# Two attention tails and the cross attention between them, written as one block

## The reference, cut to what matters

```python
def _mha(x, y, ..., causal):
    xn = _ln(x, lnx_g, lnx_b)
    yn = _ln(y, lny_g, lny_b)
    q, k, v = ...                                   # 16 heads of 32
    a = softmax(q @ k.T * D ** (-0.5)); o = a @ v   # (a masked where causal)
    x_out = x + o @ li1_w + li1_b
    h = gelu(_ln(x_out, ln3_g, ln3_b) @ li2_w + li2_b)     # 256 -> 1024
    return x_out + h @ li3_w + li3_b                       # 1024 -> 256

x = _ln(xx, ln1_g, ln1_b)
x = x + _mha(x, x, a1_..., causal=True)
x = _ln(x, ln2_g, ln2_b)
return x + _mha(x, ee, a2_..., causal=False)        # keys and values from the context
```

## Time and profile before

| what | us |
|---|---|
| median of 3 runs | 2060.34 |
| lowest, highest run | 2058.19, 2062.22 |
| the profiled execution | 2051.76 |
| its span, first to last instruction | 2050.0 |
| first tail, first matmul to the next block's first instruction | 545.88 to 696.11 |
| cross attention 2, to the second tail's first matmul | 696.11 to 805.82 |
| second tail, to the next block's first instruction | 805.82 to 956.25 |

### The profile page before, as it was taken

One profiled execution on the slowest core, in us unless ns is written; L12 is line 12 of the kernel. 1 busy time (PEld: TensorE's weight loads), 2 busy tenths in 40 slices (PEclk: granted clock), 3 DMA queues, 4 the chain that ended last, 5 costly groups with the idle time before them and its releaser, 6 DMA issues. The chain is left out here.

```text
span 2050.0 us, 32319 instructions
## 1 busy us (share of the span) xinstructions
PE 1793.4 (87%) x11428; PEld 1168.0 (57%) x11428; DVE 1281.9 (63%) x2721; ACT 1039.8 (51%) x2198; POOL 699.8 (34%) x1001
## 2 busy tenths in 40 slices
PE   6988888888899797998999989999998998871795
PEld 3445555555567466674666655556666554551795
DVE  5489999999633485233878852268787344968112
ACT  3489999999521263212676731256766111541231
POOL 0023333333423444322565531135555112450322
PEclk9999999999999899999999999999999999986897
DMA  3441111110000200021000001010000000037695
GB/s 118 153 138 43 42 43 43 43 43 2 1 1 1 62 1 1 1 63 44 1 6 6 6 9 60 0 44 4 3 6 6 20 0 16 1 106 186 186 310 164
DMA packets 104896, 101.72 MB, mean 50 GB/s; under 512 B 34896, under 2 KB 88480, under 8 KB 104608
## 3 DMA queue, kind: packets, MB, share of 16 engines
q1 hardware_dynamic: 101664, 95.31, 15.8%
q0 software_dynamic: 3072, 4.34, 1.1%
HBM read 80.60 MB, written 16.92 MB: 48 GB/s over the span
## 5 line engine op out<-in xcount | busy, mean ns | idle before, releaser
L612 DVE TENSOR_REDUCE negmax<-sps 128x1 f32<-128x1024 f32 x256 | 309.2, 1219 | 35.2 <-PE sps L534 32.7
L656 ACT ACTIVATE prob<-sps,negmax 128x1024 f32<-128x1024 f32 x256 | 287.0, 1122 | 25.0 <-DVE negmax L612 20.1
L1531 POOL TENSOR_TENSOR la_pr<-la_pr,la_ri 128x512 f32<-128x512 f32 x128 | 157.2, 1256 | 161.0 <-DVE la_ri L1594 161.0
L702 POOL TENSOR_TENSOR probT<-probT,after 128x128 f32<-128x128 f32 x256 | 116.9, 457 | 244.7 <-DVE probT L620 217.0
L1781 ACT ACTIVATE la_pr<-la_pr,la_nx 128x256 f32<-128x256 f32 x256 | 127.0, 497 | 127.7 <-DVE la_nx L1635 127.7
L534 PE MATMUL sps<-ks,qs 128*128 128x512 f16 x512 | 168.8, 381 | 17.9 <-ACT probT L668 14.0
L1966 PE MATMUL la_bs<-lf_zT,lfw 128*128 128x512 f32 x352 | 153.0, 594 | 0.0
L550 PE MATMUL tps<-ident,prob 128*128 128x128 f32 x704 | 125.0, 282 | 26.9 <-DVE probT L620 19.0
L1541 POOL TENSOR_TENSOR la_qs<-la_qn,ores 128x256 f32<-128x256 f32 x128 | 113.8, 921 | 88.9 <-DVE la_qn L1648 88.9
L550 PEld LDWEIGHTS tps<-ident,prob 128*128 128x128 f32 x704 | 81.0, 140 | 89.9 <-issue 46.1
L1966 PEld LDWEIGHTS la_bs<-lf_zT,lfw 128*128 128x128 f32 x352 | 66.4, 190 | 82.5 <-issue 82.4
(11 more groups left out here) (378 smaller groups left out, 3855.0 us busy)
## 6 DMA issues: line engine op xcount, KB each, us to landing
w1e<-in_fc_T SPq DMA_DIRECT2D x16, 1024.0 KB, 6.4
w2e<-in_fc_T SPq DMA_DIRECT2D x16, 1024.0 KB, 9.5
qs<-q_parts SPq DMA_DIRECT2D x128, 64.0 KB, 1.9
ks<-k_parts SPq DMA_DIRECT2D x128, 64.0 KB, 1.9
q_parts<-parts SPq DMA_DIRECT2D x8, 512.0 KB, 3.6
k_parts<-parts SPq DMA_DIRECT2D x8, 512.0 KB, 3.6
lfw<-in_L_ffn_w SPq DMA_DIRECT2D x6, 640.0 KB
ores<-in_L_ffn_wqkv SPq DMA_DIRECT2D x2, 1536.0 KB, 6.3
```

Of the source, the lines that this page charges most:

```text
L612: dve.tensor_reduce(negmax[:, n % 4:n % 4 + 1], slots[n % NS][:], X, ALU.max, negate=True).then_inc(s.max_done, 1)
L656: act.activation(prob[:, n % 3, :], slots[n % NS][:], ACT.Exp, bias=negmax[:, n % 4:n % 4 + 1], accum_out=rowsum[:, tile % 2, n % QUAD:n % ...
L702: pool.tensor_tensor(blk, blk, after[:], ALU.mult).then_inc(s.masked, 1)
L1531: ins = pool.tensor_tensor(prob[:, h:h + 2, :], prob[:, h:h + 2, :], rinv[:, h:h + 2].unsqueeze(2).to_broadcast([P, 2, 2 * P]), ALU.mult)
```

## The change

One function, `tails_and_cross`, takes the place of `attention_tail` (both calls) and of the call of `cross_attention` for "x2". `cross_attention` itself stays for the later stage. What it does:

- **One block.** One set-up and one clearing of semaphores, no meeting of the engines at the two seams. `s1`, `s` and `s2` are the semaphores of the first tail, the cross attention and the second tail.
- **Shared banks.** The eight PSUM banks are two pairs `sps` (tx_s) and four single ones `zbank` (tx_z), `qbank` (tx_q), `obank` (tx_o), `pbank` (tx_p). The tails' `tps` are the halves of the pairs, `p1` is zbank and qbank, `p3` is obank and pbank. The ramp's alternation between banks goes.
- **Shared buffers and weights.** The tails share one set of buffers and of weight tiles. SP loads the second tail's weights once the first tail has finished with the tiles (it waits for the last p3, sum2, base, x_out, gelu and zT of s1).
- **The ramp is dealt into the first tail's groups 2 and 3.** turn_y, keys, both values and four turn_z stand between the hidden matmuls of group 2, four projections between its project3 tiles, four turn_z in hidden of group 3, and three iterations of the ramp between the project3 tiles of group 3. `turn_y` writes zbank, which is p1's first bank, and waits for all eight x1 additions of the first tail.
- **The second tail begins in the drain.** project1(s2, 0, j) stands behind weigh at `it` = 9 to 12, two tiles of group 1 at `it` = 15, the other two behind the loop. VectorE's first_sum(s2, 0) comes in iteration 14; GpSimd's base(s2, 0, j) in iterations 8 to 11.

```diff
-        def tail_weights(phase, name, c, width=P):
+        def tail_weights(c):
...
+            def ahead(sp, sem, name, width, norm):
...
-        t2ctx = ExitStack()
-        attention_tail("t1", t1_weights, lambda t, m: ores[:, t // TPB * MC + m, t % TPB * P:(t % TPB + 1) * P], "norm")
-        t2_weights, t2_ahead = tail_weights("t2", "L0_xattn_a2_", t2ctx, 2 * D1)
-        cross_attention("x2", H1, D1, lambda t: x0res[:, t, :], ores, x2_weights, True, None, SCALE1, t2_ahead)
-        attention_tail("t2", t2_weights, lambda t, m: ores[:, t // TPB * MC + m, t % TPB * P:(t % TPB + 1) * P], "gate",
+        def tails_and_cross(weights, cross):
...
+                tps = [sps[0][:, 0:GW], sps[0][:, GW:2 * GW], sps[1][:, 0:GW], sps[1][:, GW:2 * GW]]
+                p1 = [bank[:].rearrange("p (a d) -> p a d", a=2) for bank in (zbank, qbank)]
+                p3 = [bank[:].rearrange("p (a d) -> p a d", a=2) for bank in (obank, pbank)]
...
+                        sp.wait_ge(s1.p3_done, NT)
+                        sp.wait_ge(s1.sum2, NT)
+                        sp.wait_ge(s1.base_done, NT)
+                        sp.wait_ge(s1.x_out, NT)
+                        sp.wait_ge(s1.gelu_done, G * FC)
+                        sp.wait_ge(s1.zT_done, G * KD)
+                        tail_ahead(sp, s2.w_in, "L0_xattn_a2_", 2 * D1, False)
+                        sp.wait_ge(s2.p1_done, NT)
+                        sp.wait_ge(s.next_in, attention_ahead(0)(sp, s.next_in))
...
+                        bases(s1, 0)
+                        inverse1(s1, 0)
+                        sums(s1, 0)
+                        bases(s1, 1)
+                        inverse1(s1, 1)
+                        masks()
+                        y_inverse()
+                        for g in range(2):
+                            for q in range(2):
+                                inverse2(s1, g, q)
+                            sums(s1, g + 1)
+                            bases(s1, g + 2)
+                            inverse1(s1, g + 2)
+                        for t in range(4):
+                            inverse_deviation(t)
+                        value_blocks()
+                        for t in range(4, 8):
+                            inverse_deviation(t)
+                        for q in range(2):
+                            inverse2(s1, 2, q)
+                        sums(s1, 3)
+                        for t in range(8, 12):
+                            inverse_deviation(t)
+                        for q in range(2):
+                            inverse2(s1, 3, q)
+                            inverse_deviation(12 + q)
+                        for t in range(NT):
+                            share(t)
+                            if live(t + 14):
+                                inverse_deviation(t + 14)
+                            if 8 <= t < 8 + J:
+                                base(s2, 0, t - 8)
+                            if t == NT - 2:
+                                inverse1(s2, 0)
+                        sums(s2, 0)
...
+                        hidden_input(s1, 0)
+                        hidden_input(s1, 1)
+                        y_norm()
+                        y_apply()
+                        results(s1, 0)
+                        hidden_input(s1, 2)
+                        results(s1, 1)
+                        hidden_input(s1, 3)
+                        for t in range(4):
+                            statistics(t)
+                        duplicate()
+                        normalise(0)
+                        normalise(1)
+                        values(0)
+                        values(1)
+                        key_blocks()
+                        normalise(2)
+                        normalise(3)
+                        for t in range(4, 8):
+                            statistics(t)
+                        results(s1, 2)
+                        for t in range(4, 8):
+                            normalise(t)
+                            statistics(t + 4)
+                        normalise(8)
+                        normalise(9)
+                        top(0)
+                        result(s1, 3, 0)
+                        normalise(10)
+                        statistics(12)
+                        top(1)
+                        result(s1, 3, 1)
+                        normalise(11)
+                        statistics(13)
+                        for it in range(NT):
+                            shares(it)
+                            if live(it + 2):
+                                top(it + 2)
+                            if live(it + LEAD_X + 1):
+                                normalise(it + LEAD_X + 1)
+                            if live(it + 14):
+                                statistics(it + 14)
+                            if it == NT - 2:
+                                first_sum(s2, 0)
+                        normed_sum(s2, 0)
...
+                        normed(s1, 2)
+                        for f in range(FC):
+                            gelu(s1, 2, f)
+                            if f == 0:
+                                y_out()
+                            if f == 1:
+                                keys()
+                            if f >= 4:
+                                inputs(f - 4)
+                        queries(0)
+                        queries(1)
+                        normed(s1, 3)
+                        queries(2)
+                        queries(3)
+                        for f in range(FC):
+                            gelu(s1, 3, f)
+                            if f in (2, 3, 5, 6):
+                                inputs((4, 5, 6, 7)[(2, 3, 5, 6).index(f)])
...
+                        def turn_y():
+                            pe.wait_ge(s1.x1_done, G * 2)
+                            pe.wait_ge(s.y_done, 1)
+                            pe.transpose(zbank[:, 0:P], yn[:], ident[:]).then_inc(s.y_turned, 1)
...
+                        def ramp(it):
+                            turn_z(it + LEAD_X)
+                            project(it + LEAD_Q)
+                            score(it + LEAD_S)
...
+                        for f in range(FC):
+                            hidden(s1, 2, f)
+                            if f == 0:
+                                turn_y()
+                            elif f == 1:
+                                keys()
+                            elif f < 4:
+                                values(f - 2)
+                            else:
+                                turn_z(f - 4)
+                        for j in range(J):
+                            project3(s1, 2, j)
+                            if j == J - 2:
+                                turn_sum(s1, 3)
+                            project(j)
+                        for f in range(FC):
+                            hidden(s1, 3, f)
+                            if f in (2, 3, 5, 6):
+                                turn_z((4, 5, 6, 7)[(2, 3, 5, 6).index(f)])
+                        for j in range(J):
+                            project3(s1, 3, j)
+                            if j < J - 1:
+                                ramp(j - 3)
+                        for it in range(NT + 1):
+                            if live(it - 1):
+                                turn_probs(it - 1, 0)
+                            if live(it + LEAD_X):
+                                turn_z(it + LEAD_X)
+                            if live(it + LEAD_Q):
+                                project(it + LEAD_Q)
+                            if live(it - 1):
+                                turn_probs(it - 1, 1)
+                            if live(it + LEAD_S):
+                                score(it + LEAD_S)
+                            if live(it - 1):
+                                weigh(it - 1)
+                            if 9 <= it < 9 + J:
+                                project1(s2, 0, it - 9)
+                            if it == NT - 1:
+                                project1(s2, 1, 0)
+                                project1(s2, 1, 1)
+                        project1(s2, 1, 2)
+                        project1(s2, 1, 3)
+                        turn_sum(s2, 0)
...
+        tails_and_cross(t1_weights, x2_weights)
```

769 lines of the change are left out of this document (545 added, 224 removed).

## The result

The changed kernel takes 2065.04 us (median of 10 runs, 2063.84 to 2066.7) against 2060.74 us for the kernel before in the same comparison: ratio 1.002, 95% interval 1.0011 to 1.0029, so 4 us slower (2.3 to 6.0), where 2.5 were forecast and 2062.8 us named. Two later comparisons of the same pair gave 1.0033 (1.0016 to 1.005) and 1.0037 (1.0017 to 1.0057). The profiled execution took 2064.37 us, with a span of 2062.6.

A forecast was written before the change was run, and what follows sets the result against it. TensorE's idle and slow stretches were taken as the bound. Mark one's +4.3 us and the drain's +6.9 and +3.4, against time won at the second seam, gave +2.5 on 2060.34: 2062.8 us, range 2056.5 to 2067.5.

The forecast's parts named there:

- the case's own bounds: Whole kernel, likeliest case (chance 0.64): 2059.5 to 2066 us, from both restarts, small waits and variation between runs.
- Step 1: First tail, group 2: TensorE stands 11.6 us at turn_y, waiting for all eight x1 additions.
- Step 2: Restart behind the turn_y stand: the clock is at half pace for 3.3 to 6.3 us, costing 2.3 us.
- the rule on transposes: At restarts: transposes don't count as TensorE activity that brings the clock up; by it the sum would be 0.8 us more.
- Steps 3 and 4: First tail's end at 725.3, then TensorE stands 4.7 us ahead of turn_z(11) for normalise(11), with a low clock behind.
- Mark one: When TensorE reaches turn_z(12): 736.0 against 731.68, +4.3 us, bounds +3.6 and +5.1.
- the slower rival: Groups 2 and 3: ScalarE's input pair comes late at seven turn_z, 3.5 us together, 2066.3 us; chance 0.20.
- Step 5: Drain, a closed chain: project1 comes wholly on top, 6.9 us in iterations 9 to 12, 3.4 at 15.
- Step 6: Second tail's first hidden matmul at 824.5 against 822.03, +2.5 us; only the seam's 1.6 and 0.2 are won.

The follow-up runs named there:

- e1: Changed kernel with turn_y, keys and values writing p3's banks instead of p1's, with vector work, turn_z and projections moved to suit: 2044.69 us, ratio to before 0.9967.
- e4: Changed kernel with the six project1 tiles in the drain, and group 0's x1 work, moved behind the loop: 2070.1 us, ratio to before 1.004.
- e5: Changed kernel with the project1 tiles of iterations 9 to 12 moved between the halves of turn_probs: 2058.73 us, ratio to before 1.0.
- e8: Changed kernel with other banks, VectorE's work ahead of the first tail's last result, and the drain filled with project1 and group 0's sum turn: 2036.01 us, ratio to before 0.9869.
- e7: Changed kernel with other banks for turn_y, keys and values, and VectorE's work ahead of the first tail's last result: 2046.12 us, ratio to before 0.9915.
- e6: Changed kernel with five project1 tiles directly ahead of weigh in iterations 12 to 16, three behind the loop: 2057.7 us, ratio to before 1.0.

## Why the prediction was right, step by step

The named time was 2.2 us low, inside the case's own bounds (2059.5 to 2066; the terms given for them add up to 2059.0 and 2067.0), and the side and size of each large term held. Two small ones did not, one was missing, and that the total came so near is partly luck (last point).

- **Step 1, the stand at turn_y:** 11.6 forecast, 11.42 measured; e1 shows its cause.
- **Step 2, the clock:** the granted clock, read in windows of a quarter us, was back at 652.6, 5.0 us behind the restart (3.8 and 3.9 in the two other traces). From the end of the stand to project3 of group 2 the prediction had 19.1 us (646.2 to 665.3), the trace 18.9. At the second restart two transposes and a dense projection left the clock low for 5.9 us (732.04 to 737.9: the score is at half pace too), near the long value that the prediction had from the rows; the two other traces have 4.8 and 4.7. Between executions of the same instructions this moved turn_z(12) by 0.5 us, against the 0.8 us in question, so the rows cannot decide what the rule on transposes ("TensorE: Matmul & The Clock Gate", Part 4, the Trainium skill) would add here.
- **Steps 3 and 4:** the last tile of project3 ends 0.8 us later than forecast (726.1 against 725.3; a set of tile, transposes, projection and score takes 6.68 and not 6.47); the stand was 4.53 (4.7 forecast). Then 6.48 us to turn_z(12) instead of 6.0, the low clock behind turn_z(11) costing 2.9 us where 2.4 were taken. **Mark one** is +5.4, just past its upper bound of +5.1, by these two terms. ScalarE's pair, the slower rival, is refuted: at no interleaved turn_z does TensorE stand.
- **Step 5, the drain:** 6.05 us an iteration, 6.0 forecast. That none of it would be absorbed because the idle time lies between the halves is what e4 (moved behind the loop: nothing won, nothing lost once the low clock is taken out) and e5 (moved between the halves: 4.7 us won) show from both sides. The prediction looked for a low clock only behind long stands; the one in the drain, 1.8 us in this trace, was in none of its sums.
- **Step 6, the end:** "The block's end stays as it is" failed by 1.1 us (135.35 against 134.26): 0.66 for the stand ahead of the first GELU (0.40 in the bracket and 0.26 of lost overlap), 0.43 at the clearing of the semaphores.
- **The comparison's own footing:** the profile of before that all sums started from was a lucky one in the drain (clock up) and an unlucky one at the first seam (weigh(0) at 189.4 where the other traces have 188.0). By the first traces of both the block grew by 6.7 us where 2.5 were forecast; the medians differ by 4.3 only, and the two other traces of before lose clock in the drain as well, which would explain it. So the named time came near partly because the executions of before are on the whole worse than the one that the sums started from. (The two profiled executions themselves are 12.6 us apart; 1.4 of that lies ahead of the block and 4.4 behind it, in stages that are the same in both.) With the clock's losses in the drain taken out, the changed block is 194.2 + 34.7 + 50.6 + 135.3 = 414.8 us and that of before, by its third trace, 188.0 + 34.7 + 52.1 + 134.3 = 409.1: the change costs some 5.7 us, twice the forecast, and the three ratios (4, 7 and 8 us) lie around that. Short were mark one, which against the two other traces of before is +6.1 to +6.9 and not +4.3, and the end by 1.1.

So the change as a whole traded 8.0 us of standing at the seam and a thin ramp for two stands of its own making. What the removed seams gave went to the first early writer of a shared bank and to VectorE's order behind the last result; both could be had back: with the drain filled as well, e8 is 27 us below the before of its comparison.

## What to carry to other kernels

When blocks are merged, the bank that a new early step writes decides as much as its place: ask for each whose last reader is late, before the order is fixed. A stand behind a queue of vector work goes only when every early reader of that queue is moved, not the first alone. Work put into a latency-bound drain is hidden only where TensorE waits between the links of the chain, and only as long as it waits there (1.1 us of each tile's 1.72 in e5). Whether filling these waits also keeps the clock up is likely by three traces and not proven.

## What the runs showed of the hardware

- **The clock falls in a drain without any long stand.** Ahead of the fall TensorE stands 0.77 us in each iteration, and from iteration 13 on, where no score is left, up to 1.20 us more; the clock went from 2.4 to 1.2 GHz for 3 to some 21 us in nine of the eleven traces that have a thin drain (before three times, the changed kernel three times, e1 to e4, e7), not in the first of before and in e1. In the three with project1 in the drain's waits (e5, e6, e8) it read 1.00 throughout the drain, in one trace each. e5's last iterations are as thin as e1's, and four of e5's other executions were slower at a lower mean clock, so what exactly holds the clock is left open.
- **How long a low clock lasts differs between executions of one code:** behind the same stand of 4.5 us, with the same code up to there, it was back after 5.9, 4.8 and 4.7 us in the changed kernel and after 5.0, 5.9 and 5.3 in e4, e5 and e6. In e1, whose TensorE had not stood for 11 us before, it took 2.9; one trace does not tell whether that is the code or the execution. At the first seam of before weigh(0) moved by 1.4 us from trace to trace. A profile of one execution gives the price of a low clock only to within some us, and in a thin drain not even whether the clock falls.
- **A table load can wait with the instruction it serves.** GELU's table (1.28 us) was loaded at 831.17, behind 1.64 us of idle time that ended with TensorE's first piece, and TensorE stood 0.40 us that it had not stood before. In the first tail of the same kernel it was loaded right behind the last input, at no cost. Why is left open.
